# A cap of two on the indirect transfers in flight, in place of waits for finished tiles

## The reference

```python
x = x + 0.5 * L0_ffn(layernorm(x))     # 8 experts, top 2, 128 -> 2 x 256 -> 128
x = x + L0_attn(layernorm(x))          # gated attention with squared ReLU
x = x + 0.5 * L0_ffn(layernorm(x))
x = x + 0.5 * L1_ffn(layernorm(x))     # 8 experts, top 2, 128 -> 2 x 352 -> 128
x = x + L1_attn(layernorm(x))          # causal linear attention, 16 heads
x = x + 0.5 * L1_ffn(layernorm(x))
```

```python
scores = xn @ w_router.T
top, idx = top_k(scores, 2)
up = x_of_the_row @ w_up[expert].T;  u, gate = split(up);  h = u * silu(gate)
out = sum over the two experts of weight * (h @ w_down[expert].T)  + skip
```

## Time and profile before

| | |
|---|---|
| median of 3 runs | 758.73 us (758.34 to 760.62) |
| profiled execution, span from first to last instruction | 751.7 us |
| PE (matmul) busy | 616.4 us, 82% |
| DVE busy | 404.3 us, 54% |
| ACT busy | 263.8 us, 35% |
| POOL (GpSimd) busy | 318.2 us, 42% |
| mean granted TensorE clock | 0.932 of full speed |
| DMA queue of the direct transfers | 115.79 MB, 52.6% of 16 engines |
| DMA queue of the indirect transfers | 16.79 MB, 7.4% of 16 engines |

### The profile page before, as it was taken

One profiled execution on the slowest core, in us unless ns is written; L12 is line 12 of the kernel. 1 busy time (PEld: TensorE's weight loads), 2 busy tenths in 40 slices (PEclk: granted clock), 3 DMA queues, 4 the chain that ended last, 5 costly groups with the idle time before them and its releaser, 6 DMA issues.

```text
span 751.7 us, 15429 instructions
## 1 busy us (share of the span) xinstructions
PE 616.4 (82%) x4590; PEld 567.3 (75%) x4590; DVE 404.3 (54%) x1385; ACT 263.8 (35%) x549; POOL 318.2 (42%) x352
## 2 busy tenths in 40 slices
PE   2597888959969598767879779798898989888987
PEld 1386777848759488667779779697887979877987
DVE  6744343815528146342445335297796876954446
ACT  2233342523524333322333223443634435323331
POOL 4535444261441633544350534514615736344134
PEclk9999899989989989786988889899999999998999
DMA  7578576635626347564765657475564575556853
GB/s 253 149 221 260 170 204 212 194 110 148 187 75 199 116 143 222 155 208 135 216 197 149 190 156 214 136 207 164 173 201 132 159 232 156 181 166 224 261 157 76
DMA packets 113268, 133.57 MB, mean 178 GB/s; under 512 B 10931, under 2 KB 76227, under 8 KB 112806
## 3 DMA queue, kind: packets, MB, share of 16 engines
q1 hardware_dynamic: 104998, 115.79, 52.6%
q0 software_dynamic: 8192, 16.79, 7.4%
HBM read 103.83 MB, written 28.71 MB: 176 GB/s over the span
## 4 chain that ended last, share of the span: by engine, by line
PE 59%; DVE 12%; another core or an unknown queue 12%; issue 7%; ACT 7%; POOL 2%; DMA 0%; DVEq 0%; ACTq 0%
PE up_gate L1029 18%; PE up_gate L1022 11%; PE y L983 10%; PE side L1110 3%; PE y L985 3%; PE side L1044 2%; ACT hidden L581 2%; POOL b_rstd L486 2%; PE side L1060 2%; DVE hidden L686 2%; PE side L1126 2%; ACT x_res L598 2%; DVE rms_out L708 1%; DVE kv_lo L872 1%
## 5 line engine op out<-in xcount | busy, mean ns | idle before, releaser
L686 DVE TENSOR_TENSOR hidden<-up_gate,hidden 128x256 f32<-128x256 f32 (+1 forms) x240 | 115.7, 488 | 252.0 <-ACT hidden L581 125.0
L1029 PE MATMUL up_gate<-rows_T,up 128*128 128x128 f32 x1440 | 194.5, 286 | 26.0 <-issue 14.0
L1029 PEld LDWEIGHTS up_gate<-rows_T,up 128*128 128x128 f32 x1440 | 181.4, 200 | 32.4 <-issue 19.6
L495 POOL DMA_INDIRECT rows_dram<-rms_out,rows_of x128 | 130.1, 1016 | 171.8 <-DVE rows_of L832 90.5
L581 ACT ACTIVATE hidden<-up_gate 128x256 f32<-128x256 f32 (+1 forms) x240 | 104.3, 436 | 279.8 <-PE up_gate L1022 103.0
L514 POOL DMA_INDIRECT y_rows<-y_dram,rows_of x120 | 121.9, 1016 | 85.3 <-ACT hidden L581 46.1
L1022 PE MATMUL up_gate<-rows_T,up 128*128 128x128 f32 x960 | 139.7, 291 | 16.5 <-ACT rows_T L586 9.6
L1022 PEld LDWEIGHTS up_gate<-rows_T,up 128*128 128x128 f32 x960 | 126.7, 203 | 24.7 <-issue 22.1
L983 PE MATMUL y<-down,hidden 128*128 x480 | 78.7, 288 | 8.2 <-DVE hidden L686 6.0
L486 POOL TENSOR_TENSOR b_rstd<-b_var,minus_half 128x8 f32<-128x8 f32 x16 | 26.8, 1674 | 121.6 <-DVE b_var L703 121.5
L983 PE MATMUL y<-down_a,hidden 128*128 x480 | 76.3, 283 | 0.0
(11 more groups left out here) (188 smaller groups left out, 700.4 us busy)
## 6 DMA issues: line engine op xcount, KB each, us to landing
up<-in_up SPq DMA_DIRECT2D x120, 352.0 KB
up<-in_up SPq DMA_DIRECT2D x120, 256.0 KB
rows<-rows_dram SPq DMA_DIRECT2D x47, 256.0 KB, 3.0
y_dram<-y_tile SPq DMA_DIRECT2D x45, 256.0 KB, 2.5
rows_dram<-zeros SPq DMA_DIRECT2D x12, 256.0 KB, 3.6
rows<-rows_dram SPq DMA_DIRECT2D x16, 192.0 KB
y_dram<-y_tile SPq DMA_DIRECT2D x15, 192.0 KB
rows_dram<-rms_out,rows_of POOLq DMA_INDIRECT x128
```

Of the source, the lines that this page charges most:

```text
L495: pool.indirect_dma_start(out=xg_d[g], out_offset=bass.IndirectOffsetOnAxis(ap=pos[g][:, at:at + 1], axis=0), in_=xs(Z, GROUPS[g][c // TB] ...
L686: dve.tensor_tensor(h, u, h, ALU.mult).then_inc(mult_done, 1)
L1029: last = pe.matmul(U[q % 3][:, c * P:(c + 1) * P], upW[n % RING][:, at + c * P:at + (c + 1) * P], rows_, start=True, stop=True)
```

## The change

`pace` goes. The indirect transfers are put into two lanes: the first of each pair is lane 0, the second lane 1. Each lane has semaphores of its own, and before a transfer is issued GpSimd waits until the previous transfer of its lane, which is the one two places ahead, has landed; this holds across scatters and gathers and for `gather_early` as well. Those who wait for a whole block (SyncE in `load_rows`, VectorE in `combine`) wait for both lanes.

```diff
-        scattered = [sem(f"scattered{g}") for g in range(NG)]
+        scattered = [[sem(f"scattered{g}_{k}") for k in range(2)] for g in range(NG)]
-        gathered = [[sem(f"gathered{b}_{h}") for h in range(2)] for b in range(NB)]
+        gathered = [[[sem(f"gathered{b}_{h}_{k}") for k in range(2)] for h in range(2)] for b in range(NB)]
...
-                sp.wait_ge(scattered[g], 16 * 2 * CH[g] * turns(s, g))
+                sp.wait_ge(scattered[g][0], 16 * CH[g] * turns(s, g))
+                sp.wait_ge(scattered[g][1], 16 * CH[g] * turns(s, g))
...
-            def pace(t):
-
-                if 1 < t <= SLOTS:
-                    pool.wait_ge(silu_done, t - 1)
+            flight = [None, None]
+
+            def lane_free(k):
+
+                if flight[k] is not None:
+                    pool.wait_ge(*flight[k])
...
-                    pace(t)
-                    for at in (2 * c, 2 * c + 1):
+                    for k2 in range(2):
+                        at = 2 * c + k2
+                        lane_free(k2)
                         pool.indirect_dma_start(out=xg_d[g], out_offset=bass.IndirectOffsetOnAxis(ap=pos[g][:, at:at + 1], axis=0),
                                                 in_=xs(Z, GROUPS[g][c // TB], c % TB * P, P), in_offset=None,
-                                                bounds_check=TILES[g] * P - 1, oob_is_err=False).then_inc(scattered[g], 16)
+                                                bounds_check=TILES[g] * P - 1, oob_is_err=False).then_inc(scattered[g][k2], 16)
+                        flight[k2] = (scattered[g][k2], 16 * (CH[g] * (turns(s1, g) - 1) + c + 1))
...
-                    pace(t)
                     i = TB * GROUPS[g].index(b) + c
                     for k2 in range(2):
                         at = 2 * i + k2
+                        lane_free(k2)
...
-                                                bounds_check=TILES[g] * P - 1, oob_is_err=False).then_inc(gathered[b][c // 2], 16)
+                                                bounds_check=TILES[g] * P - 1, oob_is_err=False).then_inc(gathered[b][c // 2][k2], 16)
+                        flight[k2] = (gathered[b][c // 2][k2], 16 * (2 * s + c % 2 + 1))
...
-                    dve.wait_ge(gathered[b][h], 16 * TB * (s + 1))
+                    for k2 in range(2):
+                        dve.wait_ge(gathered[b][h][k2], 16 * 2 * (s + 1))
```

More of the change, by code:

```diff
@@ L530, in gather_early @@
                     at = 2 * c + k2
+                    lane_free(k2)
                     pool.indirect_dma_start(out=gath[b % 2][:, (TB * k2 + c) * P:(TB * k2 + c + 1) * P], out_offset=None,
                                             in_=early_d, in_offset=bass.IndirectOffsetOnAxis(ap=early_pos[:, at:at + 1], axis=0),
-                                            bounds_check=(LATE + 1) * P - 1, oob_is_err=False).then_inc(gathered[b][c // 2], 16)
+                                            bounds_check=(LATE + 1) * P - 1, oob_is_err=False).then_inc(gathered[b][c // 2][k2], 16)
+                    flight[k2] = (gathered[b][c // 2][k2], 16 * (2 * s + c % 2 + 1))
             def attention(l, j, ka):
```

## The result

The changed kernel takes **769.01 us** (median of 4 runs, 765.16 to 771.85), the kernel before 759.67 us beside it (758.34 to 769.52). The ratio is 1.0133, 95% interval 1.0089 to 1.0178: **slower by 1.3%**, where 731 us and a gain were forecast. Some executions of a kernel are slow ones, at a lower granted clock; the ratios leave them out and the medians don't, and all but one execution of experiment 10 (718.5 us), its profiled one too, and all but two of experiment 15 (658.7 and 665.7 us) are slow. The span of the profiled execution is 767.8 us and its own time 769.48 us, so 1.7 us lie around a span. The 7.0 us that the prediction took for that were too many: the profiled execution of before must have taken about 751.7 + 1.7 = 753.4 us, an estimate, 5 us under its median.

The account below looks back on a forecast made before the run. TensorE's signals, held during close indirect transfers, were taken to cost 88 us of the chain. From 758.7 us, -30 (holds) - 6 (clock) + 7 (later scatters) + 1 (added waits) = -28 us gave 731 us; range 694 to 784 us.

Parts of the forecast that it names:

- What bounds the kernel: Chain that ended last: TensorE's signals are held up while indirect transfers follow closely, 88 us or 11.7% of the span.
- (a): Lane waits on GpSimd: landing taken as 3.0 us, so 0.44 us more for each pair of transfers.
- (b): Holds of TensorE's signals: of 88 us, 58 us stay (64 pairs at 0.90 us), so -30 us.
- The cap frees TensorE wholly: Rival: nearly all of the 88 us and the clock come back, 673 us; chance 8%.
- (c): TensorE's granted clock after the hold: 2 us back at each of three blocks, -6 us (0 to -7.5).
- (d): Scatters end later, on the path only at SyncE's five waits, GpSimd's queued lines included: +7 us (0 to 37).
- (e): Removal of `pace`, which ended 86.0 us of GpSimd's idle time: costs 0 with holds short, more with holds long.
- (f): Added waits of SyncE and VectorE for both lanes, at five places: 0 to 1.5 us, taken as +1 us.
- The hold outlasts the cap: Rival: a hold once begun lasts until GpSimd's run of transfers is over, so slower, 784 us; chance 28%.
- The lanes never wait: Rival: transfers land in under 2.56 us everywhere, so only `pace` is removed, 774 us; chance 4%.
- The hold has another cause: Rival: signals are stuck for a reason other than the runs of transfers, nothing won there, 767 us; chance 4%.

Follow-up runs that it names:

- experiment 10: The changed kernel with a cap of three transfers in place of two, on chip 9: 737.1 us, with the kernel before at 762.0 us.
- experiment 15: The kernel before, `pace` kept, with one small GpSimd write added behind each pair of transfers, on chip 13: 667.3 us, with the kernel before at 645.1 us.
- experiment 9: The kernel before with `pace` taken out and no cap put in, on chip 9: 794.3 us, ratio 1.044.
- experiments 7: The kernel before without `pace` and without a cap, with three small GpSimd writes behind each pair of transfers, on chip 9: 782.5 us, ratio 1.039.
- experiment 8: The changed kernel with the cap on the scatters alone, gathers waiting for no landing, on chip 9: 750.3 us, ratio 0.993.
- experiment 1: The kernel before with `pace` taken out and no cap put in, on chip 14: 644.2 us, ratio 0.997.

## Why the prediction was wrong

The forecast had the gain at a third of its size (36 us against 110) and the price at a fifteenth (8 us against 125). The measured time lies inside the stated range, but on the side of a loss, for a reason that none of the rivals had.

- **What bounds the kernel: right.** The 88 us of the chain were TensorE's signals, held while GpSimd issues indirect transfers back to back. They are 0 after the change, and on chips without holds the kernel before takes 645 to 647 us. With the clock and what follows, the holds are worth some 110 us, if nothing else differs between the chips; that the changed kernel takes 769 to 770 us on both kinds speaks for it.
- **(a), the lane wait: mis-sized.** The landing was right: 3.0 us taken, 2.98 measured (median over 256, by the packets). Left out was what follows a landing. In the chain after, the wait ends at 156.27 + 3.78 = 160.05 us and the next transfer starts at 160.82, 0.77 us later; from the end of the packets to that start it is 1.1 us (median of the waits). Without a wait the whole step from one issue to the next is 0.30 us. A pair takes (17.78 - 13.37) / 3 = 1.5 us more in a block, where 0.44 us stood.
- **(b), the hold: mis-sized.** 58 us were said to stay. It is 2.9 us over the silus. The rival *The cap frees TensorE wholly*, given 8%, had this part right.
- **(c), the clock: right at its place, wrong in sum.** The clock of 166 to 172 us went from 0.53 to 1.00. But over the span the mean granted clock fell from 0.932 to 0.911: TensorE now has waits of up to 10.9 us for the normalised rows elsewhere.
- **(d), the step that failed.** It said "It is on the path only where SyncE waits for it: 5 times", and counted what is queued behind the waiting transfers (L486, L538, L547) inside 7 us. Those five waits were read in a kernel whose bound was TensorE. With the holds gone TensorE could be done 110 us sooner, and then the queue of GpSimd, with 32 blocks one behind another, is the next bound: each us added to a block costs 0.7 to 0.9 us. 32 x 4.4 = 141 us on the queue are some 125 us, not 7. Its upper bound of 37 us was no bound, since it too took five places.
- **(e), `pace`: right both ways.** With holds short it costs nothing (644 against 647 us without holds; with the cap 775 with it, 770 without). With long holds its removal costs 794 against 762 us, 32 us where the rival had 18.
- **(f): not seen apart**; nothing in the waits after names it.
- **The rivals.** *The hold outlasts the cap* describes experiment 9 (one hold of 10.0 us that ends with the run), not the change: the cap's gaps end it. *The lanes never wait* is refuted by 166 us of such waits. *The hold has another cause* is refuted by experiments 7, 8 and 9: fewer or more transfers close behind one another, fewer or more stuck signals; but whether there are holds at all depends on the chip. The rule of the Trainium skill's page SBUF — State Buffer (Who interferes with whom), that DMA doesn't contend with a compute engine, agrees with chips 13 and 14 (nothing stuck) and does not describe chip 9 or that of the case (81 and 87 us stuck in the kernel before). The Trainium skill's page DMA: Bandwidth & Descriptors (Anatomy of one DMA — SWDGE (gpsimd) path), with its about 2.0 us of fixed time, is near the quickest transfers here, 1.87 us to the end of their packets, and a third short of the median of 2.98 us; the measured times decide.

In sum: -110 (holds and clock) + 125 (queue) = +15 us against +9 measured in the case and +14 on chip 9.

## What to carry to other kernels

When a change takes a stall off the bounding engine, price its side effects against the next bound, not against the waits of the profile at hand: here GpSimd, busy for 42% of the span, became the bound once TensorE ran freely and the waits for landings stood on its queue, since the chains of all blocks pass through it. Here a wait for a landing on GpSimd's queue cost the landing, then 1.1 us to the start of the next transfer, and it delayed everything queued behind it. Where transfers must be spaced, a short gap without a wait did better (710.5 against 762.0 us on chip 9), though it loses 3.6% on chip 14, which has no holds; the kernel should be timed on more than one chip before either is kept.

## What the runs showed of the hardware that was not expected

- The same kernel takes 645 to 647 us on two chips (13 and 14) and 756 to 762 us on chip 9 and that of the case. On the latter silus start up to 7.2 us late (10.0 us in experiment 9) because of TensorE's completion signals, while GpSimd issues indirect transfers with gaps of 0.3 us; without `pace` chip 14 has the same gaps (experiment 1) and no stuck silu. Why chips differ in this is not known from these runs.
- With gaps of 0.70 us between pairs the longest hold was 3.9 us, with 1.6 us and more about 1 us, with 0.49 us 6.3. Fewer transfers were out at once too, so the gap alone is not shown to be the cause.
- In experiment 8 the capped scatters had 1.6 us of stuck silus behind them and the uncapped gathers 47.3.
